# The start of the two feed-forward phases: order of the second unit's pair, the weight pieces and the third unit's normalise

## What is computed

```python
x = x + attn_a(layernorm(x))     # causal softmax attention, 2 heads of 128, partly rotated q and k
x = x + ffn(layernorm(x))        # h = silu(x wg^T) * (x wu^T); h wd^T; hidden size 768
x = x + attn_b(layernorm(x))     # linear attention with decay, 8 heads of 64, sigmoid gate
x = x + ffn(layernorm(x))        # the same three weights again
```

## Time and profile before

| what | value |
|---|---|
| median of 3 runs | 1916.81 us |
| the profiled execution's own time | 1915.64 us |
| its span | 1913.9 us |
| TensorE matmul | busy 1875.6 us, 98% of the span |
| VectorE / ScalarE / GpSimd | 69% / 46% / 27% |
| chain that ended last | TensorE 89%, VectorE 4%, SP's queue 2% |
| `ff1` on TensorE | from 540.43 us to about 821 us |
| `ff2` on TensorE | from 1617.86 us to the end |

### The profile page before, as it was taken

The page is one execution under the profiler, slowest core; times in us unless marked ns, Lnnn a source line. Parts: engine busy times, 40 slices in busy tenths (PEclk is TensorE's granted clock), DMA queues, the critical chain, the costliest instruction groups (busy, mean ns, idle before and its releaser), DMA issues.

```text
span 1913.9 us, 36549 instructions
## 1 busy us (share of the span) xinstructions
PE 1875.6 (98%) x12321; PEld 1620.0 (85%) x12321; DVE 1325.4 (69%) x3141; ACT 879.4 (46%) x1716; POOL 519.6 (27%) x453
## 2 busy tenths in 40 slices
PE   7999999999999999999999999999999999899998
PEld 6888888888788888888888888888888887788887
DVE  6666566655677888766666666676667677778885
ACT  6666656665644444453333333333333332444443
POOL 5313202320321232132322222222222223422210
PEclk9999999999999999999999999999999999999999
DMA  7100000000022112220000000000000001222332
GB/s 251 33 1 0 0 0 0 0 0 0 12 63 46 29 29 32 34 66 12 13 10 10 9 9 9 10 11 11 11 11 11 12 12 18 38 62 62 64 59 53
DMA packets 230614, 53.19 MB, mean 28 GB/s; under 512 B 209680, under 2 KB 228752, under 8 KB 230160
## 3 DMA queue, kind: packets, MB, share of 16 engines
q1 hardware_dynamic: 229280, 49.53, 12.8%
q10 hardware_dynamic: 1264, 2.76, 0.4%
HBM read 18.69 MB, written 8.39 MB: 14 GB/s over the span
## 4 chain that ended last, share of the span: by engine, by line
PE 89%; DVE 4%; issue 2%; SPq 2%; POOL 1%; ACT 1%; DMA 0%; ACTq 0%; DVEq 0%; POOLq 0%
PE PS L323 18%; PE PS L1169 16%; PE PS L1178 9%; PE PS L332 7%; PE PS L855 7%; PE PS L826 6%; PE PS L1633 5%; PE PS L1675 4%; PE PS L1619 3%; PE PS L844 3%; PE PS L1652 3%; PE PS L866 2%; PE PS L1639 2%; SPq L271 2%; PE PS L1607 1%
## 5 line engine op out<-in xcount | busy, mean ns | idle before, releaser
L323 PE MATMUL PS<-ln_xh,lin_w 128*128 128x512 f32 x768 | 248.8, 392 | 0.0
L1106 ACT ACTIVATE ff_silu<-PS 128x512 f32<-128x512 f32 x192 | 114.5, 597 | 235.2 <-PE PS L1169 207.1
L1390 POOL TENSOR_TENSOR lin_yg_lo<-stage,lin_yg_hi 128x512 fp32r<-128x512 f32 x64 | 82.3, 1286 | 484.1 <-ACT lin_yg_hi L1408 484.1
L1141 DVE SCALAR_TENSOR_TENSOR ff_h<-PS,ff_silu 128x512 f32<-128x512 f32 x192 | 131.3, 685 | 111.3 <-PE PS L1169 93.5
L1408 ACT ACTIVATE lin_yg_hi<-stage 128x512 fp32r<-128x512 f32 x64 | 40.5, 632 | 347.0 <-DVE stage L1503 315.7
L323 PEld LDWEIGHTS PS<-ln_xh,lin_w 128*128 128x128 f32 x768 | 144.2, 188 | 28.7
L1125 DVE TENSOR_TENSOR ff_h_lo<-ff_h,ff_h_hi 128x512 fp32r<-128x512 f32 x192 | 168.2, 876 | 0.4
L564 POOL TENSOR_TENSOR qk<-qk,swapped 64x128 f32<-64x128 f32 (+2 forms) x96 | 96.5, 1005 | 243.0 <-DVE swapped L708 237.2
L1465 DVE TENSOR_TENSOR lin_AD<-PS,lin_decay 128x512 f32<-128x512 f32 x128 | 82.2, 684 | 104.6 <-PE PS L1619 104.6
L855 PE MATMUL PS<-probT,v_a 128*128 128x128 f32 x1152 | 153.4, 278 | 0.0
L855 PEld LDWEIGHTS PS<-probT,v_a 128*128 128x128 f32 x1152 | 139.5, 192 | 14.4 <-ACT probT L628 7.4
(11 more groups left out here) (172 smaller groups left out, 5183.8 us busy)
## 6 DMA issues: line engine op xcount, KB each, us to landing
ff_raw<-ln_xn SPq DMA_DIRECT2D x480, 32.0 KB, 2.0
ln_xl<-ln_xn SPq DMA_DIRECT2D x288, 32.0 KB, 1.9
out_x<-X SPq DMA_DIRECT2D x16, 512.0 KB, 2.9
X<-in_x SPq DMA_DIRECT2D x7, 1024.0 KB, 5.5
stage<-in_w_lin SPq DMA_DIRECT2D x1, 2048.0 KB, 8.2
stage<-in_w_gate SPq DMA_DIRECT2D x2, 768.0 KB, 7.4
stage<-in_w_up SPq DMA_DIRECT2D x2, 768.0 KB, 8.9
stage<-in_w_down SPq DMA_DIRECT2D x2, 768.0 KB, 10.2
```

The costliest lines, as they stand in the source:

```text
L323: last = nc.tensor.matmul(out, w, x, start=n == 0, stop=n == len(terms) - 1)
L1106: nc.scalar.activation(silu[:, f % NB_GU, :], PS[:, f % NB_GU, :], ACT.Silu, scale=W_SCALE).then_inc(silu_done.sem, 1)
L1141: nc.vector.scalar_tensor_tensor(h[:, f % 2, :], PS[:, NB_GU + f % NB_GU, :], W_SCALE, silu[:, f % NB_GU, :], ALU.mult, ALU.mult).then_inc ...
```

## The change

It edits where and when the first units of the two feed-forward phases are prepared.

- `front.raw` and the odd pair of `ff1` are allocated first, ahead of `w_lo`, so they lie where attention's q, k, v weights were. SP's wait for `a_scores_end` is removed. In `ff2`, unit 1 lands in the first 1024 columns of the low gate and up weights, which are free when the last projections have ended (`lin_projected_end`).
- ScalarE makes the high half of unit 1 first of all in unit 0 (`f == 0`), ahead of the first SiLU; in `ff2` it also waits for `lin_decayed_end`.
- GpSimd makes the low half of unit 1 ahead of all weight work. The cast of `ff1` is cut into eighteen pieces of 256 columns. In `ff2` the low gate and up weights (twelve pieces) move from the end of linear attention into unit 0, behind `pool_low`; the low down weights follow (six pieces). `pool_rstd` of unit 2 goes ahead of the last `gated_low`.
- VectorE normalises unit 2 at the end of the phase in front, ahead of the last residual, and makes its block transpose one slice earlier.
- `raw` of `Turned`'s methods becomes the buffer itself. Other allocations only change place.

```diff
--- before.py
+++ after.py
@@ -258,9 +258,9 @@
 
     def landing(self, par, raw):
 
-        return self.raw[:] if raw else self.parts[par][1][:].bitcast(F32)
-
-    def sp_move(self, sp, unit, par, raw=False):
+        return self.parts[par][1][:].bitcast(F32) if raw is None else raw
+
+    def sp_move(self, sp, unit, par, raw=None):
 
...
@@ -510,7 +510,6 @@
         O, Y = PS[:, 6, 0:P], PS[:, 7, 0:M]
         low_row = PS[0:1, 6, P:2 * P]
 
-        env["a_scores_end"] = s_ready.sem, s_ready.at(NB - 1, NS)
         env["a_out_end"] = y_ready.sem, y_ready.at(NB - 1, NS)
         env["a_x_end"] = y_done.sem, y_done.at(NB - 1, NS)
 
@@ -780,6 +779,7 @@
                 out_low(b, NS - 1)
                 residual(b, NS - 2)
                 if last:
+                    following.ln.dve_normalise(dve, 2)
                     residual(b, NS - 1)
 
@@ -960,6 +960,8 @@
         sb = lambda n, shape, dt=F32: ctx.enter_context(nc.sbuf_tensor(f"{name}_{n}", shape, dt))
         parts_of_w = [slice(0, KT * FF), slice(KT * FF, 2 * KT * FF), slice(2 * KT * FF, NW)]
         if nth == 1:
+            front.raw = sb("raw", [P, KT, UN])
+            front.parts[1] = sb("odd_xh", [P, KT, UN], F32R), sb("odd_xl", [P, KT, UN], F32R)
             w_hi, w_lo = env["ff_w_hi"][:], sb("w_lo", [P, NW], F32R)[:]
             gate_up_lo, lo_of_down = w_lo[:, 0:2 * KT * FF], w_lo[:, parts_of_w[2]]
@@ -967,21 +969,19 @@
         gu = lambda w, n: w[:, parts_of_w[n]].rearrange("p (k f) -> p k f", k=KT)
         gate_hi, up_hi, gate_lo, up_lo = gu(w_hi, 0), gu(w_hi, 1), gu(gate_up_lo, 0), gu(gate_up_lo, 1)
         ln = front.ln
-        front.parts[1] = sb("odd_xh", [P, KT, UN], F32R), sb("odd_xl", [P, KT, UN], F32R)
-        NB_GU = 3
-        if nth == 1:
-            front.raw = sb("raw", [P, KT, UN])
+        NB_GU, NH, LAG = 3, 4, 3
+        h_lo = sb("h_lo", [P, NH, UN], F32R)
         silu = sb("silu", [P, NB_GU, UN])
         if nth == 2:
             front.raw = sb("raw", [P, KT, UN])
+            front.parts[1] = sb("odd_xh", [P, KT, UN], F32R), sb("odd_xl", [P, KT, UN], F32R)
+        first_raw = front.raw[:] if nth == 1 else gate_up_lo[:, 0:KT * UN].bitcast(F32).rearrange("p (k t) -> p k t", k=KT)
         h = sb("h", [P, 2, UN])
+        h_hi = sb("h_hi", [P, NH, UN], F32R)
         if nth == 2:
             lo_of_down = sb("down_lo", [P, NF * M], F32R)[:]
         down_hi, down_lo = (w.rearrange("p (k m) -> p k m", k=NF) for w in (w_hi[:, parts_of_w[2]], lo_of_down))
         sx = [front.pair(0), front.pair(1)]
-        NH = 4
-        h_hi, h_lo = sb("h_hi", [P, NH, UN], F32R), sb("h_lo", [P, NH, UN], F32R)
-        LAG = 3
 
         prep_hi, prep_lo = signals.prep_hi, signals.prep_lo
         gate_ready, up_ready, down_done = signals.gate_ready, signals.up_ready, signals.down_done
@@ -1011,6 +1011,10 @@
 
             return (NF * par + f) % NH
 
+        def landing_of(first, left):
+
+            return (first_raw if first else front.raw[:]) if left else None
+
         def next_of(u, par, left):
 
             if left:
@@ -1034,13 +1038,13 @@
                 if upcoming:
                     nfront, nu, npar = upcoming
                     if left:
-                        if first:
-                            sp.wait_ge(*env["a_scores_end" if nth == 1 else "lin_decayed_end"])
-                        else:
+                        if first and nth == 2:
+                            sp.wait_ge(*env["lin_projected_end"])
+                        if not first:
                             wait_alone(sp, front.lo_done.sem, front.lo_done.at(u, 1), front.sp_passed)
                     else:
                         wait_alone(sp, up_ready.sem, up_ready.at(u - 1, NF), front.sp_passed)
-                    nfront.sp_move(sp, nu, npar, raw=bool(left))
+                    nfront.sp_move(sp, nu, npar, raw=landing_of(first, left))
                 if following and isinstance(u, int) and u == 1:
                     sp.wait_ge(prep_lo, 2)
                     load_lin_weights(sp, env, io)
@@ -1060,23 +1064,34 @@
         @block.gpsimd
         def _(pool):
 
+            def low_pieces(lo, part):
+                raw, hi = stage[:, part], w_hi[:, part].bitcast(F32)
+                for at in range(0, part.stop - part.start, M):
+                    piece = slice(at, at + M)
+                    last = nc.gpsimd.tensor_tensor(lo[:, piece], raw[:, piece], hi[:, piece], ALU.subtract)
+                last.then_inc(prep_lo, 1)
+
             def unit(u, par, first, left):
                 upcoming, after = next_of(u, par, left), after_next(u, left)
+                if first:
+                    front.pool_low(pool, u + 1, 1, raw=first_raw)
                 if first and nth == 1:
                     pool.wait_ge(*env["a_out_end"])
-                    nc.gpsimd.tensor_copy(w_lo, stage[:, 0:NW]).then_inc(prep_lo, 2)
+                    for f in range(3 * NF):
+                        at = slice(f * M, (f + 1) * M)
+                        last = nc.gpsimd.tensor_copy(w_lo[:, at], stage[:, at])
+                    last.then_inc(prep_lo, 2)
                 if first and nth == 2:
-                    pool.wait_ge(*env["lin_decayed_end"])
-                    raw, hi = stage[:, parts_of_w[2]], w_hi[:, parts_of_w[2]]
-                    for f in range(NF):
-                        at = slice(f * M, (f + 1) * M)
-                        last = nc.gpsimd.tensor_tensor(lo_of_down[:, at], raw[:, at], hi[:, at].bitcast(F32), ALU.subtract)
-                    last.then_inc(prep_lo, 1)
+                    pool.wait_ge(prep_hi, 2 * NF + 1)
+                    pool.wait_ge(front.lo_done.sem, front.lo_done.at(u + 1, 1))
+                    low_pieces(gate_up_lo, slice(0, 2 * KT * FF))
+                    pool.wait_ge(*env["lin_gated_end"])
+                    low_pieces(lo_of_down, parts_of_w[2])
                 if after and not first:
                     after[0].ln.pool_rstd(pool, after[1])
-                if upcoming:
+                if upcoming and not first:
                     nfront, nu, npar = upcoming
-                    nfront.pool_low(pool, nu, npar, raw=bool(left))
+                    nfront.pool_low(pool, nu, npar, raw=landing_of(first, left))
 
             def lin_low(n):
                 at = bass.ds(n * LIN_PIECE, LIN_PIECE)
@@ -1096,11 +1111,13 @@
             def unit(u, par, first, left):
                 upcoming = next_of(u, par, left)
                 for f in range(NF):
-                    if f == (2 if first else NF - 2) and upcoming:
+                    if f == (0 if first else NF - 2) and upcoming:
                         nfront, nu, npar = upcoming
                         if left and not first:
                             act.wait_ge(up_ready.sem, up_ready.at(u - 1, NF))
-                        nfront.act_high(act, nu, npar, raw=bool(left))
+                        if first and nth == 2:
+                            act.wait_ge(*env["lin_decayed_end"])
+                        nfront.act_high(act, nu, npar, raw=landing_of(first, left))
                     act.wait_ge(gate_ready.sem, gate_ready.at(u, f + 1))
                     act.wait_ge(h_done.sem, h_done.at(u, f - NB_GU + 1))
                     nc.scalar.activation(silu[:, f % NB_GU, :], PS[:, f % NB_GU, :], ACT.Silu,
@@ -1149,9 +1166,9 @@
                             after[0].ln.dve_tile_stats(dve, after[1], range(UT))
                         if f == 1 and not first:
                             after[0].ln.dve_aggregate(dve, after[1])
-                        if f == (1 if first else 3):
+                        if f == 3 and not first:
                             after[0].ln.dve_normalise(dve, after[1])
-                        if f == (2 if first else 4):
+                        if f == (1 if first else 4):
                             after[0].dve_blocks(dve, after[1], (front, u + 1))
                 if not left:
                     low_part(u, par, NF - 1)
@@ -1273,6 +1290,8 @@
                                                      signals.yg_lo_done)
         env["lin_decayed_end"] = ad_done.sem, ad_done.at(NB - 1, 2 * NC)
         env["lin_quotients_end"] = y_done.sem, y_done.at(NB - 1, 2 * NC)
+        env["lin_projected_end"] = proj_ready.sem, proj_ready.at(NB - 1, NHALF * NITEM)
+        env["lin_gated_end"] = yg_done.sem, yg_done.at(NB - 1, NC)
         env["lin_x_end"] = x_done.sem, x_done.at(NB - 1, NC)
 
         def next_of(b, half, last):
@@ -1335,15 +1354,11 @@
                         if last and half == NHALF - 1:
                             if c == 0:
                                 ff2_high()
-                            if c == 2:
-                                ff2_low(0)
                     if first and half == NHALF - 1:
                         ff_float()
                 if last:
+                    following.ln.pool_rstd(pool, 2)
                     gated_low(b, TB - 1)
```

(14 more changed lines are left out.)

5 lines of the change are left out of this document (2 added, 3 removed).

## The result

The changed kernel takes 1920.83 us in the median (1918.82 to 1924.79, 20 runs) against 1915.81 (1913.62 to 1918.74, 20 runs) for the kernel before in the same comparison: ratio 1.0029, 95% interval 1.0022 to 1.0036. The profiled execution took 1920.2 us, 4.6 more than the one before (1915.64); its span is 4.5 us longer.

What follows compares the result with a forecast made beforehand. It took TensorE's waits in each feed-forward phase's first units as the bound. 3.15 - 2.35 + 4.2 - 0.4 = +4.6 us gave 1920.2 on the profiled execution, 1921.4 with the median 1.17 above; range 1914.5 to 1924.8.

Steps and rivals of the forecast that it cites:

- Step 1: SP's move of unit 1: the removed wait does not hold SP, the block transpose does; gain nothing, cost nothing.
- Step 2: ScalarE's high half first in unit 0: its landing wait stalls TensorE 5.4 and 5.3 us; +3.15 first phase, -2.35 second.
- Step 3: TensorE's clock after the two new stalls falls to the low level: 2.1 us each, +4.2 us together.
- Step 4: GpSimd's pair before the weight pieces, pieces for one cast: the 4.18 us go, counted in ScalarE's term; otherwise 0, bound +1.
- Step 5: VectorE's normalise of unit 2 moved to the phase in front: covered by the stall, cost 0; otherwise 0 to 3.46 us per phase.
- Step 6: Wait for unit 3's pair: its move starts later, clear of the next weights' load; between 0 and -1.3, taken -0.4 us.
- (b): Rival, first units of both phases: early pair and free head wait, -8.7 us, 1908.1 us; chance 0.12.
- (a): Rival, TensorE after the stalls: ScalarE waits but the clock costs little, +0.4 to +3.3 us, 1917.2 to 1920.1; chance 0.28.
- (c): Rival, TensorE after each stall: low clock for all of 8.3 us, another 2.0 each, 1925.4 us; chance 0.10.

Runs made afterwards that it cites:

- the first experiment: The changed kernel with ScalarE's high half of unit 1 put back ahead of the third slice in both phases: 1908.61 us, ratio 0.9966.
- the old normalise: The changed kernel with ScalarE's high half back in third place in both phases, and the normalise of unit 2 back in unit 0: 1910.49 us, ratio 0.9974.
- a slice later: Changed kernel, unit 1's high half ahead of the fourth slice in both phases, unit 2's block transpose after the third product: 1908.74 us, ratio 0.9967.

## Why the prediction was right

The forecast was 1921.4 us, and +4.6 on the profiled execution; measured were 1920.83 and +4.6. The mechanism is the one that was forecast, but the closeness of the number is in part luck. The places that the sum names went up by 5.26 + 0.37 + 0.26 = +5.9, and 1.4 us less outside them (the end of the program, the start of the first phase), which no step had, brought it back. The forecast's base of 1916.81, a median of three, was also 1.0 us above the median of twenty; from median to median the change costs 5.0.

**Step 1** (SP's waits, nothing): right. With the old waits the time is the same.

**Step 2** (ScalarE's head wait, stalls of 5.4 and 5.3 us): right in place, releaser and size, 5.60 and 5.54. The edit alone in the kernel before gives the same stall in the first phase, and taken out of the changed kernel it gives 12 us back. Unit 0 of the first phase rose by 5.26, forecast 3.15 for the wait and 2.1 for the clock; the clock took 1.8, so the wait was 0.3 more, and the two misses cancel.

**Step 3** (clock, 2.1 us per stall): right. The round behind the stall (eight gate and up matmuls, eight downs) took 4.60 and 5.24 us against 2.79 for a free one: a loss of 1.81 us in the first phase and 2.45 in the second, together 4.3. The clock had fallen when TensorE resumed, 0.50 over the first 3.1 us, and was back for the downs of that round in the first phase and for the next round in the second. In the first phase the dummies confirm it with 1.78 us of unit 0.

The second phase is the term that was off: units 0 and 1 together were forecast at -2.35 + 2.1 = -0.25 us and are +0.37. That is within 0.7 us of it, made up of a clock loss of 2.45 in place of 2.1 and a stall of 5.54 in place of 5.3.

**Step 4** (pair ahead, pieces for one cast): right that the 4.18 us go and that the pieces cost nothing beside the stall. They took 7.63 us in the first phase (allowed: 8.1) and 15.3 in the second (estimated: 14). Two things it did not say: without the stall the eighteen pieces are late for unit 3 (1.24 us of wait, unit 2 at 19.20), and the cast in pieces is worth some 1.3 us of unit 0 in the profiles, 1.05 of it in waits for the two low halves.

**Step 5** (normalise moved, nothing beside the stall): right, 1.38 and 2.34 us hidden. In a kernel without the stall it may be worth up to 2 us, of which the profile shows 0.1 as waiting.

**Step 6** (unit 3's pair, -0.4): wrong, no gain: +0.10 and +0.16. I took that unit 3's move would start later against the load of the weights and so be shorter. In the first phase it starts 17.63 us behind the first matmul of unit 1 in the kernel before and in the changed one alike, so a shift of unit 1 changes nothing for it. What does change the wait is the longest of SP's sixteen issues: 1.90 us in the kernel before (wait 1.30), 2.00 in the changed one (1.39), 1.22 in the first experiment (0.65), 0.85 with the dummies in both phases (0.28). In the second phase it starts 17.62 us behind unit 1 in the changed kernel too; slow matmuls in unit 1 (19.07 in the kernel before) or GpSimd's late pieces (18.93 in the first experiment) put it off.

The rivals: (b), the faster outcome, named the landing as its deciding point, and it was some 6 us too late in both phases, as worked out. Of (a), a fall that costs little, the windows at 0.50 say no. Of (c), 8.3 us of low clock, they say no as well: matmuls are at 0.40 us again 4.6 us behind the resumption in the first phase and 5.2 in the second.

The drain that the Trainium skill (ScalarE: Activation LUTs, What ACT_TABLE_LOAD costs) adds to a switch of tables would have cost 2.8 us more. It does not show here: the load starts 0.02 us after the copy ends (550.54 to 550.56), and the SiLU at the load's end. By the Trainium skill (TensorE: Matmul & The Clock Gate, Part 1) the engine goes to the lower of its two levels after idleness; the trace agrees, with 0.50 after 5.6 us of idle time and 1.00 where dummy matmuls filled it.

What the prediction did not do is ask the other way: it summed the change as one. The edits around ScalarE's are worth 6.4 us by themselves, and one digit hid them.

## What to carry to other kernels

An instruction that waits for a transfer belongs in an in-order queue at the place where its data is due, not at the place where it would be nice to have it; everything behind it inherits the wait, and here that was a table load and the two SiLUs TensorE was to live on. Before moving work ahead, compare the landing with the start of what is displaced (550.1 against 543.6): the sign of this change stood in these two numbers. When a change with several good parts comes out slower, put back one part at a time, because the good parts stay hidden by the bad one (6.4 us of gain under a loss of 12 here); and after each gain look at the next unit for the wait that took its place. Before a difference of 1 or 2 us between two profiles is put down to an edit, look at the granted clock behind each wait and at the longest issue of each move: both differ between executions by as much.

## What was not expected of the hardware

- A stall costs more than its length: behind 5.6 and 5.5 us of idle time TensorE's granted clock was 0.50 from the first matmul, and each cost another 1.8 and 2.45 us. Twenty-two useless matmuls in its place win that back.
- Much shorter waits can cost the clock too, and need not. It fell behind waits of 1.81 us (the old normalise), 1.97 us (the high half back in the first phase alone) and 2.15 us (a slice later), and stayed at 1.00 behind 1.72 and 2.03 us in the first experiment. One and the same wait at the end of linear attention, 2.07 or 2.08 us, left it at 1.00 in the kernel before and in the changed one, and was followed by 0.50 in the runs with the dummies in both phases and with the slice later. Each fall in unit 0 of the first phase cost 1.5 us, nearly as much again as the wait. What decides was not found.
- SP's issues of the 32 KB block transfers take 0.61 us each, but in the first moves of a phase there is, in nearly every run, a longer one among the sixteen, of up to 2.00 us. In the kernel before, the one of 1.90 us stands in the chain of waits (start, duration, queue, line), in the third move of the first phase:

```profile
579.35 1.90 SPq L271
```

The run with the dummy matmuls in both phases had none in two of its three moves of the second phase, and the landings behind them came 0.8 to 1 us earlier. The cause was not found.
- VectorE's subtraction with both inputs in SBUF waits for the end of a running GpSimd instruction, but gets in between two of them: behind the 4.49 us cast it took 3.70 us, while VectorE's product, which reads one input from PSUM, took its usual 0.69 us beside the same cast; in the changed kernel, beside pieces of 0.42 us, the same operation took 0.94:

```profile
553.93 0.94 DVE L1142 TENSOR_TENSOR ff_h_lo<-ff_h,ff_h_hi 128x512 fp32r<-128x512 f32 x1
```

The pieces cost GpSimd more in all (7.63 us for 18 against 4.04 for one cast), which is a good trade where GpSimd has the time.
